# Attention and ternary feed-forward on one core: loads and angle tables of chunk 0 reordered, sums directly behind their values

## The chip, the cores and the metric

The kernel runs on one core of a Trainium2 chip. The metric is the device time of one execution in microseconds (us). The engines are TensorE (PE; weight loads are listed apart as PEld), VectorE (DVE), ScalarE (ACT), GpSimd (POOL) and SyncE (SP), which here only issues DMAs; ScalarE issues some too.

## The reference

```python
xn = layernorm(x)                            # x: 2048 x 256, no scale, no shift
q, k, v = xn@Wq, xn@Wk, xn@Wv                # 8 query heads, 2 key/value heads, 32 wide
q, k = rope(q), rope(k)                      # angles from tables over the 2048 rows
std = softmax(causal(q@k.T * 32**-0.5)) @ v
qp, kp = q[..., :3]@dirs, k[..., :3]@dirs    # one number per row and head
geo = softmax(causal(qp[:, None]*kp[None, :])) @ v
attn = (std + head_scales*(geo - std)) @ Wo
z = xn @ ternary(W_syn).T + b_syn            # 1024 wide; ternary: mean(|W|)*{-1,0,1}
hidden = where(z >= 102nd largest of the row, relu(z), 0)
ffn = layernorm(xn + hidden@ternary(W_out).T + b_out)*gamma + beta
out = x + attn + ffn
```

## The kernel before

The 2048 rows are cut into four chunks of 512 rows, four tiles of 128 each. Nothing is looped at run time. `build_plan` lists every piece of work with an engine, a length, what it needs, and a rank; then it repeatedly takes, among the pieces that could start within `SLACK` (120 ns) of the first, the one of lowest rank. The result is a written order for each of the five engines' queues. `LANDING` and `done` are its assumed landing times of DMAs; they set the order and no time on the chip. Each engine works through its queue in order and waits on semaphores.

For each chunk: statistics of x (`stat`, `eps`, `shift`, L1010 to L1027), normalised rows (`xn`, L836), their transposes (`xT`, `xnT`), three projections with the rope halves of queries and keys kept apart (`qA`, `qB`, `qK`, L1291) and the values (L1295). The cosines and sines come as tables of 16 and 32 numbers a row. `spread_angles` (L555 to L564) repeats them over the heads, in three pieces a chunk; TensorE transposes a piece (`tT`, four transposes, L1276), ScalarE copies it out (`t_put`, L827). Chunk 0's pieces go to `trig`; those of the later chunks go to `trig_next`, are parked in DRAM (`t_park`, L593) and come back (`trig_in`, L599) when the ropes of the chunk before are done. The angles, the given weights, the spread pieces and `trig_next` lie in `probs`, the buffer of the exponentials, so all trig work ends before the first exponential.

The rope products (L1065 to L1072) and the joins (L1078, L736, L739) give queries and keys, which are split into a high and a low part (`khi`, `hi` on ScalarE; `klo`, `lo` on VectorE, L1088 and L1093), parked in DRAM and read back as stacks (L627, L630) of 96 rows. From them come the pieces of the row maxima (`S`, L1312; reduced on VectorE, L1126 and L1129), a transpose (`mT`) and the maxima (`m`), which go into the stack as two more rows. The geometric scores need only small rows: `gx` (L1303, L1304), `geo_hi`, `geo_lo`, the running maxima (`scan`, `geo_top`), and some 22 small DMAs.

Attention goes by slots: chunk, kind (geometric first, then standard), group of four heads, key block of 128. A slot is two pairs of scores (L1395, L1399), two exponentials (L889) into one of two halves of `probs`, on the diagonal two cuts (L746), then values (`val`, L1413) and sums (`sum`, L1420), both column-tiled into `acc`. The exponentials of slot n+2 wait for the sums of slot n. Ranks are 12 for scores, 13 for values, 12.5 for sums. Two PSUM banks (`side`) serve everything else; row-maximum pieces may also use the four score banks while no scores can run. In the order that results, 120 of the 160 sums have other work between them and their values, and TensorE enters column-tiled work 172 times (counted in the order that `build_plan` writes).

The feed-forward weights are made ternary early (`w_abs`, `wsum`, `w_cut`, `wT`, `w_put`), W_out after W_syn in the same buffer (`w_next`, L679). The feed-forward tiles (`z`, `sign`, `pick`, `hT`, `fo`, `y`) fill gaps and run mostly beside chunks 2 and 3.

## Time and profile before

| | |
|---|---|
| device time, median of 3 | 775.68 us (774.01 to 776.37) |
| the profiled execution, its own time | 776.62 us |
| its span in the trace | 774.9 us |
| busy, share of the span | PE 90%, DVE 64%, ACT 58%, POOL 29% |
| granted TensorE clock, mean | 0.927 of full |
| DMA moved | 35.46 MB |

The busy time of an engine is the time in which one of its instructions ran. The granted clock is a share of full speed: 1.0 is 2.4 GHz, 0.5 is 1.2 GHz. In a timeline a row gives start, length, engine, line, operation, written and read tile, shapes and count, and in brackets the idle time before it with what ended it. A matmul's length contains its fill and drain, so start-to-start times are read for what it costs. Consecutive like instructions are merged into one row.

### The profile page before, as it was taken

How to read it: one execution, taken by the hardware profiler on the slowest of the kernel's cores; microseconds unless marked ns; L12 is line 12 of the kernel's file. 1: busy time of each engine (PE TensorE's matmuls, PEld its weight loads, DVE VectorE, ACT ScalarE, POOL GpSimd, SP SyncE). 2: the span in 40 equal slices, each digit the busy share in tenths (PEclk: the TensorE clock that was granted, in tenths of full speed). 3: DMA queues.
4: the chain of work that ended last, by engine and by line, in shares of the span. 5: the costliest groups of instructions: out<-in, count | busy, mean ns of one | idle time of the engine just before them, and what ended most of it. 6: DMA issues, size and time to landing. Idle time of an engine off the chain costs nothing.

```text
span 774.9 us, 12300 instructions
## 1 busy us (share of the span) xinstructions
PE 694.9 (90%) x4424; PEld 327.5 (42%) x4424; DVE 498.3 (64%) x974; ACT 449.4 (58%) x733; POOL 226.8 (29%) x304
## 2 busy tenths in 40 slices
PE   0857988799999999969999999999999989998993
PEld 0533444334244443423343444554544445654532
DVE  3782786856675876558567696567665567767602
ACT  1655345344334442468444445799989989996550
POOL 3431314531111212111010120452343453247232
PEclk9965899679899998989999999999989999999996
DMA  9494038240000000160000000000000000000000
GB/s 238 150 280 134 1 128 209 77 102 1 1 7 1 1 1 1 32 158 1 0 3 3 1 1 3 22 22 28 28 22 22 28 22 28 16 22 8 1 1 27
DMA packets 26931, 35.46 MB, mean 46 GB/s; under 512 B 7090, under 2 KB 21298, under 8 KB 26483
## 3 DMA queue, kind: packets, MB, share of 16 engines
q1 hardware_dynamic: 21874, 33.80, 15.0%
q10 hardware_dynamic: 4992, 0.84, 0.6%
q8 instruction: 36, 0.59, 0.3%
q14 instruction: 29, 0.23, 0.1%
HBM read 20.08 MB, written 13.89 MB: 44 GB/s over the span
## 4 chain that ended last, share of the span: by engine, by line
PE 62%; DVE 10%; issue 5%; ACT 3%; POOL 3%; DMA 3%; SPq 1%; DVEq 0%; ACTq 0%; POOLq 0%
PE acc L1420 14%; PE acc L1413 14%; PE side L1312 10%; PE scores L1395 7%; DVE piece_max L1126 4%; PE scores L1399 3%; DMA q_stack<-q_parked 3%; PE side L1366 2%; PE side L1357 2%; PE side L1374 2%; PE side L1367 2%; ACT probs L889 2%; PE side L1349 2%; PE side L1350 1%; POOL probs L746 1%
## 5 line engine op out<-in xcount | busy, mean ns | idle before, releaser
L889 ACT ACTIVATE probs<-scores 128x1024 f32<-128x1024 f32 (+3 forms) x320 | 271.0, 893 | 230.9 <-PE acc L1420 208.3
L1126 DVE TENSOR_REDUCE piece_max<-side 128x1 f32<-128x512 f32 x189 | 125.3, 685 | 78.9 <-PE side L1312 77.5
L1413 PE MATMUL acc<-probs,v_nat 128*32 128x512 f32 (+3 forms) x1280 | 158.1, 568 | 8.7 <-POOL probs L746 8.5
L1420 PE MATMUL acc<-probs,ones_all 128*32 128x512 f32 (+3 forms) x1280 | 156.8, 564 | 0.0
L1312 PE MATMUL side<-k_stack,q_stack 96*128 96x512 f32 (+3 forms) x309 | 122.5, 450 | 17.0 <-DMA q_stack<-q_parked 9.2
L746 POOL TENSOR_SCALAR_AFFINE_SELECT probs<-probs 128x256 f32<-128x256 f32 x128 | 60.8, 484 | 243.8 <-ACT probs L889 242.5
L1312 PEld LDWEIGHTS side<-k_stack,q_stack 96*128 96x128 f32 x309 | 55.5, 199 | 106.2 <-issue 52.4
L1395 PE MATMUL scores<-q_stack,k_stack 98*128 98x512 f32 (+3 forms) x320 | 92.5, 393 | 1.5 <-ACT probs L889 1.3
L1129 DVE CUSTOM_DVE_ANT_0 side<-side,tail_mask 128x256 f32<-128x256 f32 (+3 forms) x120 | 57.7, 488 | 33.3 <-PE side L1312 32.8
L1413 PEld LDWEIGHTS acc<-probs,v_nat 128*32 128x32 f32 x1280 | 37.2, 114 | 86.9 <-issue 64.8
L1152 DVE RECIPROCAL d_raw<-d_raw 128x512 f32<-128x512 f32 x16 | 53.6, 3347 | 23.2 <-ACT o_raw L902 23.2
L1395 PEld LDWEIGHTS scores<-q_stack,k_stack 98*128 98x128 f32 x320 | 54.0, 194 | 33.6 <-ACT probs L889 23.8
L1399 PE MATMUL scores<-q_geo,k_geo 10*128 10x512 f32 (+3 forms) x320 | 58.0, 485 | 5.9 <-ACT probs L889 4.9
L1420 PEld LDWEIGHTS acc<-probs,ones_all 128*32 128x32 f32 x1280 | 29.9, 111 | 48.5 <-issue 45.7
L1399 PEld LDWEIGHTS scores<-q_geo,k_geo 10*128 10x128 f32 x320 | 23.6, 190 | 47.5 <-ACT probs L889 31.2
L785 POOL TENSOR_TENSOR y_rstd<-y_mv,minus_half 128x1 f32<-128x1 f32 x16 | 9.6, 600 | 106.5 <-DVE y_mv L1258 106.5
L1276 PE MATMUL side<-ident,probs 128*128 128x128 f32 x48 | 11.6, 403 | 25.4 <-ACT probs L559 18.8
L1247 DVE TENSOR_TENSOR h_split<-side,h_split 128x512 fp32r<-128x512 f32 x32 | 21.2, 681 | 18.8 <-ACT h_split L980 18.8
L1240 DVE SCALAR_TENSOR_TENSOR work<-z_buf,thresh 128x1024 f32<-128x1024 f32 x16 | 22.0, 1378 | 17.4 <-DVEq L1237 17.4
L1366 PE MATMUL side<-down_T,h_split 128*128 128x256 f32 x128 | 31.9, 288 | 1.0 <-DVE h_split L1247 1.0
L1367 PE MATMUL side<-down_T,h_split 128*128 128x256 f32 x128 | 30.9, 280 | 0.0
L1349 PE MATMUL side<-up_T,xs_hi 128*128 128x512 f32 x64 | 28.3, 442 | 0.5 <-DVE xs_lo L1184 0.3
(165 smaller groups left out, 911.1 us busy)
## 6 DMA issues: line engine op xcount, KB each, us to landing
q_stack<-q_parked SPq DMA_DIRECT2D x12, 512.0 KB, 8.0
q_parked<-turned SPq DMA_DIRECT2D x8, 512.0 KB, 3.0
trig_parked<-probs SPq DMA_DIRECT2D x3, 768.0 KB, 5.2
trig<-trig_parked SPq DMA_DIRECT2D x3, 768.0 KB, 4.3
res<-in_L_attn_x_dram SPq DMA_DIRECT2D x4, 512.0 KB, 8.9
x_parked<-xn SPq DMA_DIRECT2D x4, 512.0 KB, 3.2
xT_parked<-xnT SPq DMA_DIRECT2D x4, 512.0 KB, 5.2
xb<-x_parked SPq DMA_DIRECT2D x16, 128.0 KB, 2.0
```

What stands on the lines that cost most here:

```text
L746: nc.gpsimd.affine_select(out=tri, in_=tri, compare_op=ALU.is_ge, fill=0.0, base=0, pattern=[[0, 2], [1, P]], channel_multiplier=-1).then_ ...
L889: nc.scalar.activation(probs[:, slot % 2, pair, :, off:], scores[:, pair, :, off:], ACT.Exp, scale=ATT_SCALE if kind == 0 else 1.0).then_i ...
L1126: free(nc.vector.tensor_reduce(piece_max[:, h, p:p + 1], pt, AX.X, ALU.max), ("S",) + a)
L1129: free(nc.vector.tensor_tensor_reduce(pt[:, 0:ncol], pt[:, 0:ncol], tail_mask[:, CHUNK - ncol:], 1.0, -3.0e38, ALU.add, ALU.max, piece_max ...
L1152: nc.vector.reciprocal(d_raw[:], d_raw[:]).then_inc(recip_ready, 1)
L1312: last = nc.tensor.matmul(pt[:, 0:ncol], q_stack[0:STK, b, h, col:col + P], k_stack[0:STK, h // HG, CHUNK * p:CHUNK * p + ncol], start=Tru ...
L1366: nc.tensor.matmul(pt[:, 0:C], h_hi[:, i], down_T[:, i], start=(i == 0), stop=False)
L1367: last = nc.tensor.matmul(pt[:, 0:C], h_lo[:, i], down_T[:, i], start=False, stop=(i == NN - 1))
L1395: last = nc.tensor.matmul(dst[:, off:], k_stack[:, g, P * j:P * j + P], q_stack[:, b, HG * g + h, off:], start=True, stop=True)
L1399: last = nc.tensor.matmul(dst[:, off:], k_geo[rows, P * j:P * j + P], q_geo[rows, g, off:], start=True, stop=True)
L1413: nc.tensor.matmul(acc[D * h:D * h + D, 0, off:], v_nat[:, j, g], probs[:, slot_no[a] % 2, h // 2, h % 2, off:], start=(j == 0), stop=(j = ...
L1420: last = nc.tensor.matmul(acc[D * h:D * h + D, 1, off:], ones[:, 0:D], probs[:, slot_no[a] % 2, h // 2, h % 2, off:], start=(j == 0), stop ...
```

## The change

Five edits, most of them in `build_plan`. Loads: the weights are issued first on ScalarE, then the angles of chunk 0 alone; SyncE issues x of chunk 0 and the small table, waits for the weights, and then issues the rest. Tables: `angles` has its own buffer of one chunk, refilled by `ang_in` (two DMAs on SyncE) for each later chunk; the spread pieces lie in the key part of `turned`, so they wait until the chunk before is parked; every chunk's pieces go straight to `trig`, and the parked trig, its DMAs and `trig_next` are gone. Sums: their rank is -1, so a sum is taken right behind its values, and row-maximum pieces find their place at the scores only. The cut of w_cut in two: `w_mean` makes mean and thresholds and frees the bank, `w_cut` the ternary matrix, with a new semaphore `ternary_ready`. Order: geo work and the statistics from chunk 2 on wait for maxima; W_out, `xz_in` and `xb_in` come behind the stack of chunk 0; W_out's thresholds come behind its maxima.

```diff
-LANDING = {"m_dma": 2300, "geo_dma": 2300, "geo_rows": 2300, "w_next": 5000, "t_park": 3500, "trig_in": 3000, "xn_park": 3500,
+LANDING = {"m_dma": 2300, "geo_dma": 2300, "geo_rows": 2300, "w_next": 5000, "ang_in": 2500, "xn_park": 3500,
...
+SUM_RANK = -1
...
+W_UNIT = 1.5
...
+        if c:
+            add("ang", "sp", 2, ("ang_in", c), 1100, [("unit", "tT", c - 1, 2)])
...
-            rank = 0 if c == 0 else 0.5
-            add("spread", "act" if c == 0 else "pool", rank, ("spread", c, s), 650 if c == 0 else 1300, [("tables",)] + turned[-2:-1])
+            rank = 0 if c == 0 else 2 * c - 0.5
+            slots_free = [("khi_park", c - 1), ("klo_park", c - 1)] if c else []
+            add("spread", "act" if c == 0 else "pool", rank, ("spread", c, s), (650, 650, 900)[s] if c == 0 else (700, 700, 900)[s],
+                [("ang_in", c)] + turned[-2:-1] + slots_free)
...
-            add("trig", "act", rank, ("t_put", c, s), 600, [("unit", "tT", c, s)] + [("t_park", c - 1)] * (c > 1), empties=("tT", c, s))
+            add("trig", "act", rank, ("t_put", c, s), 600, [("unit", "tT", c, s)] + [("rope", c - 1, k) for k in "ABK"] * (c > 0),
+                empties=("tT", c, s))
...
-        if c:
-            add("t_park", "sp", 0, ("t_park", c), 550, [("t_put", c, s) for s in range(3)])
-    add("w_sort", "dve", 0, ("w_sort",), 2000, [("w",)])
+    add("w_sort", "dve", 0.2, ("w_sort",), 2000, [("w",)])
...
-            add("stat", "dve", STAT_RANK if c else 0, ("stat", t), 650, [("x", c)])
+            add("stat", "dve", STAT_RANK if c else 0, ("stat", t), 650, [("x", c)] + [("m", c - 2)] * (c > 1))
...
-        if c:
-            add("trig_in", "sp", 1, ("trig_in", c), 550, [("t_park", c)] + [("rope", c - 1, s) for s in "ABK"])
...
-            add("rope", "dve", 0 if c == 0 else ROPE_RANK, ("rope", c, s), 1250, [("unit", "q" + s, c)] + ([("trig_in", c)] if c else [("t_put", 0, s) for s in range(3)]) + parked,
+            add("rope", "dve", 0 if c == 0 else ROPE_RANK, ("rope", c, s), 1250, [("unit", "q" + s, c)] + [("t_put", c, i) for i in range(3)] + parked,
...
+        due = [("m", c - 1)] if c else []
...
-        add("geo", "dve", rank, ("geo_lo", c), 1220, [("geo_hi", c)] + old)
-        add("geo", "dve", rank, ("scan", c), 2800, [("geo_in", c)] + old)
+        add("geo", "dve", rank, ("geo_lo", c), 1220, [("geo_hi", c)] + old + due)
+        add("geo", "dve", rank, ("scan", c), 2800, [("geo_in", c)] + old + due)
...
-            add("w", "sp", 0, ("w_next",), 500, [("w_cut", 0)])
+            add("w", "sp", 0, ("w_next",), 500, [("w_cut", 0), ("stack_lo", 0)])
...
-        unit("w", 0, ("wsum", m), 60, [("w_abs", m)])
-        add("w", "dve", W_RANK, ("w_cut", m), 4400, [("unit", "wsum", m)] + [("w_put", 0, 3)] * m, empties=("wsum", m))
+        unit("w", W_UNIT, ("wsum", m), 60, [("w_abs", m)])
+        add("w", "dve", 2, ("w_mean", m), 560, [("unit", "wsum", m)] + [("m", 0)] * m, empties=("wsum", m))
+        add("w", "dve", W_RANK, ("w_cut", m), 3900, [("w_mean", m)] + [("w_put", 0, 3)] * m)
...
-            unit("w", 0, ("wT", m, i), 440, [("w_cut", m)])
+            unit("w", W_UNIT, ("wT", m, i), 440, [("w_cut", m)])
...
-        add("xz", "sp", 3, ("xz_in", t), 550, [("xnT_park", c)] + [("xs_lo", t - 2)] * (t > 1))
+        add("xz", "sp", 3, ("xz_in", t), 550, [("xnT_park", c), ("stack_lo", 0)] + [("xs_lo", t - 2)] * (t > 1))
...
-        add("xb", "sp", 3, ("xb_in", t), 550, [("xn_park", c)] + [("y", t - 2)] * (t > 1))
+        add("xb", "sp", 3, ("xb_in", t), 550, [("xn_park", c), ("stack_lo", 0)] + [("y", t - 2)] * (t > 1))
...
-                + ([("sum",) + slots[n - 2]] if n >= 2 else [("t_park", NCH - 1), ("w_sort",)]))
+                + ([("sum",) + slots[n - 2]] if n >= 2 else [("w_sort",)]))
...
-        add("val", "pe", 12.5, ("sum", c, g, kind, j), 15 + 860 * share, [("val", c, g, kind, j)], "columns")
+        add("val", "pe", SUM_RANK, ("sum", c, g, kind, j), 15 + 860 * share, [("val", c, g, kind, j)], "columns")
...
-    done = {("x", 0): 5500.0, ("x", 1): 11000.0, ("x", 2): 13500.0, ("x", 3): 15500.0, ("tables",): 9000.0, ("dir_in",): 14000.0}
-    done.update({("w",): 9000, ("late",): 24000, ("w_in", 0): 19000, ("w_in", 1): 19000})
+    done = {("x", 0): 5200.0, ("x", 1): 13000.0, ("x", 2): 19000.0, ("x", 3): 21000.0, ("ang_in", 0): 9500.0, ("dir_in",): 14000.0}
+    done.update({("w",): 11000, ("late",): 26000, ("w_in", 0): 18000, ("w_in", 1): 19000})
...
+        angles = sb("angles", [P, TPC, ANG])
+        spread = turned[:, :, 2].rearrange("p b (t m) -> p b t m", m=P)
...
-        angles = flat[:, 0:NT * ANG].rearrange("p (t a) -> p t a", a=ANG)
-        w_given = flat[:, NT * ANG:NT * ANG + KC * QKV].rearrange("p (k n) -> p k n", k=KC)
-        trig_next = flat[:, 3 * CHUNK:6 * CHUNK].rearrange("p (s t) -> p s t", s=3)
-        spread = flat[:, 6 * CHUNK:8 * CHUNK].rearrange("p (b t m) -> p b t m", b=2, m=P)
+        w_given = flat[:, 0:KC * QKV].rearrange("p (k n) -> p k n", k=KC)
...
-        trig_parked = nc.dram_tensor("trig_parked", [NCH, P, 3, CHUNK], F32, kind="Internal").ap()
...
-        trig_out = sem("trig_out")
-        trig_in = sem("trig_in")
...
+        ternary_ready = sem("ternary_ready")
...
-            buf, tiles = spread[:, spread_no[(c, s)] % 2], slice(TPC * c, TPC * c + TPC)
+            buf = spread[:, spread_no[(c, s)] % 2]
...
-                            angles[:, tiles, at:at + HALF, None].broadcast_to([P, TPC, HALF, H]))
+                            angles[:, :, at:at + HALF, None].broadcast_to([P, TPC, HALF, H]))
...
-                 angles[:, tiles, 0:HALF, None].broadcast_to([P, TPC, HALF, G]))
+                 angles[:, :, 0:HALF, None].broadcast_to([P, TPC, HALF, G]))
...
-                        angles[:, tiles, :, None].broadcast_to([P, TPC, ANG, G]))
+                        angles[:, :, :, None].broadcast_to([P, TPC, ANG, G]))
...
+            sp.dma_start(small[:], small_table.broadcast_to([P, H * 3 + RANKS])).then_inc(dir_in, 16)
+            sp.wait_ge(w_in, N_W_IN)
...
-            sp.dma_start(small[:], small_table.broadcast_to([P, H * 3 + RANKS])).then_inc(dir_in, 16)
...
-                if k == "t_park":
+                if k == "ang_in":
...
-                    for s in range(3):
-                        consumed(sp, ("tT", c, s))
-                    sp.dma_start(trig_parked[c], trig_next).then_inc(trig_out, 16)
-                if k == "trig_in":
-                    c = key[1]
-                    sp.wait_ge(trig_out, 16 * c)
-                    for s in "ABK":
-                        consumed(sp, ("q" + s, c - 1))
-                    sp.dma_start(trig[:], trig_parked[c]).then_inc(trig_in, 16)
+                    sp.wait_ge(side_full, unit_no[("tT", c - 1, 2)] + 1)
+                    rows = slice(CHUNK * c, CHUNK * c + CHUNK)
+                    sp.dma_start(angles[:, :, 0:HALF], cos_table[rows, 0:HALF].rearrange("(t p) d -> p t d", p=P)).then_inc(ang_in, 16)
+                    sp.dma_start(angles[:, :, HALF:], sin_table[rows].rearrange("(t p) d -> p t d", p=P)).then_inc(ang_in, 16)
...
-                    consumed(sp, ("wsum", 0))
+                    sp.wait_ge(ternary_ready, 1)
...
-                    pool.wait_ge(ang_in, 32)
+                    pool.wait_ge(ang_in, 32 * (c + 1))
+                    pool.wait_ge(hi_out, 32 * c)
+                    pool.wait_ge(lo_out, 32 * c)
...
-            act.dma_start(angles[:, :, 0:HALF], cos_table[:, 0:HALF].rearrange("(t p) d -> p t d", p=P)).then_inc(ang_in, 16)
-            act.dma_start(angles[:, :, HALF:], sin_table.rearrange("(t p) d -> p t d", p=P)).then_inc(ang_in, 16)
...
+            act.dma_start(angles[:, :, 0:HALF], cos_table[0:CHUNK, 0:HALF].rearrange("(t p) d -> p t d", p=P)).then_inc(ang_in, 16)
+            act.dma_start(angles[:, :, HALF:], sin_table[0:CHUNK].rearrange("(t p) d -> p t d", p=P)).then_inc(ang_in, 16)
...
-                    if c > 1:
-                        act.wait_ge(trig_out, 16 * (c - 1))
-                    free(nc.scalar.copy(trig[:, s] if c == 0 else trig_next[:, s], pt), ("tT",) + a)
+                    if c >= 1:
+                        for q_ in ("qA", "qB", "qK"):
+                            consumed(act, (q_, c - 1))
+                    free(nc.scalar.copy(trig[:, s], pt), ("tT",) + a)
...
-                        act.wait_ge(trig_out, 16 * (NCH - 1))
...
-                        consumed(act, ("wsum", 0))
+                        act.wait_ge(ternary_ready, 1)
...
-                        consumed(act, ("wsum", 1))
+                        act.wait_ge(ternary_ready, 2)
...
-            mark(nc.vector.memset(other[KROWS:, 2], 0.0))
...
-                    if c == 0:
-                        for i in range(3):
-                            consumed(dve, ("tT", 0, i))
-                    else:
-                        dve.wait_ge(trig_in, 16 * c)
+                    for i in range(3):
+                        consumed(dve, ("tT", c, i))
+                    if c >= 1:
...
+                if k == "w_mean":
+                    m = a[0]
+                    pt = filled(dve, ("wsum", m))
+                    free(nc.vector.tensor_scalar(w_scale[:, m:m + 1], pt[:, 0:1], 1.0 / (N * C), None, ALU.mult), ("wsum", m))
+                    consumed(dve, ("wsum", m))
+                    link(nc.vector.tensor_scalar(w_cut[:, 0:1], w_scale[:, m:m + 1], 1e-8, 0.5, ALU.add, ALU.mult))
+                    link(nc.vector.tensor_scalar(w_cut[:, 1:2], w_cut[:, 0:1], -1.0, None, ALU.mult))
...
-                    pt = filled(dve, ("wsum", m))
...
-                    link(nc.vector.tensor_scalar(w_scale[:, m:m + 1], pt[:, 0:1], 1.0 / (N * C), None, ALU.mult))
-                    link(nc.vector.tensor_scalar(w_cut[:, 0:1], w_scale[:, m:m + 1], 1e-8, 0.5, ALU.add, ALU.mult))
-                    link(nc.vector.tensor_scalar(w_cut[:, 1:2], w_cut[:, 0:1], -1.0, None, ALU.mult))
+                        dve.wait_ge(down_in, 16)
+                    else:
+                        dve.wait_ge(up_in, 16)
...
-                    free(nc.vector.scalar_tensor_tensor(w_neg, w_raw, w_cut[:, 0:1], w_neg.bitcast(F32), ALU.is_gt,
-                                                        ALU.subtract), ("wsum", m))
+                    nc.vector.scalar_tensor_tensor(w_neg, w_raw, w_cut[:, 0:1], w_neg.bitcast(F32), ALU.is_gt,
+                                                   ALU.subtract).then_inc(ternary_ready, 1)
...
-                        consumed(pe, ("wsum", m))
+                        pe.wait_ge(ternary_ready, m + 1)
```

## Rows read from the trace of the kernel before

**Rows 1.** The page's part 1: busy us, share of the span, instructions.
```profile
PE 694.9 (90%) x4424; PEld 327.5 (42%) x4424; DVE 498.3 (64%) x974; ACT 449.4 (58%) x733; POOL 226.8 (29%) x304
```

**Rows 2.** Stages: window, length, busy us of each engine, granted clock, DMA share, GB/s.
```profile
0.00:65.00 65.00, 31.78 (x121) 20.68 (x121) 41.76 (x93) 28.69 (x51) 22.98 (x32) 0.84 0.78 228
...
98.50:133.20 34.70, 30.28 (x165) 15.08 (x161) 26.38 (x40) 17.09 (x28) 12.93 (x15) 1.00 0.59 163
...
175.00:490.00 315.00, 302.22 (x1843) 127.86 (x1845) 218.37 (x426) 149.34 (x204) 48.47 (x77) 0.95 0.05 13
490.00:700.00 210.00, 202.56 (x1468) 103.44 (x1468) 135.34 (x258) 191.00 (x367) 86.28 (x108) 0.98 0.08 24
```

**Rows 3.** Timeline of ScalarE, the first spread.
```profile
18.05 1.14 ACT L559 COPY probs<-probs 128x512 f32<-128x512 f32 x2 [4.20 <-DMA probs<-in_sin_table_dram]
```

**Rows 4.** Timeline of VectorE, 0 to 50 us.
```profile
5.19 0.43 DVE L1016 BATCH_NORM_STATS2 stats<-res 128x6 f32<-128x256 f32 x1 [0.21 <-DMA res<-in_L_attn_x_dram]
...
20.38 0.71 DVE L1032 COPY w_qkv<-probs 128x256 f32<-128x256 f32 x2 [12.31 <-DMA probs<-in_L_attn_Wv_dram]
...
35.10 0.69 DVE L1068 TENSOR_TENSOR turned<-side,trig 128x512 f32<-128x512 f32 x1
...
41.42 2.58 DVE L1171 SCALAR_TENSOR_TENSOR h_split<-z_buf,w_cut,h_split 128x2048 fp32r<-128x2048 f32 x1
...
44.52 1.21 DVE L1093 TENSOR_TENSOR turned<-turned 128x1024 fp32r<-128x1024 f32 x1
```

**Rows 5.** Timeline of TensorE, 28 to 65 us.
```profile
28.68 3.01 PE L1291 MATMUL side<-xnT,w_qkv 128*128 128x512 f32 x4
33.08 3.70 PE L1291 MATMUL side<-xnT,w_qkv 128*128 128x512 f32 x8 [1.38 <-DVE turned L1066]
...
41.43 1.91 PE L1304 MATMUL side<-turned,dirs_k 6*40 6x512 f32 x2
...
48.87 0.66 PE L1276 MATMUL side<-ident,probs 128*128 128x128 f32 x4
...
64.26 0.44 PE L1312 MATMUL side<-k_stack,q_stack 96*128 96x128 f32 x1 [2.92 <-DMA q_stack<-q_parked]
```

**Rows 6.** DMA issues: count, KB each, median us from issue to landing.
```profile
q_stack<-q_parked SPq DMA_DIRECT2D x12, 512.0 KB, 8.0
...
z_buf<-in_L_ffn_W_out_dram SPq DMA_DIRECT2D x1, 1024.0 KB, 5.3
...
probs<-in_sin_table_dram ACTq DMA_DIRECT2D x1, 256.0 KB, 16.7
...
probs<-in_L_attn_Wv_dram ACTq DMA_DIRECT2D x1, 64.0 KB, 8.7
```

**Rows 7.** Groups of instructions by line: busy us, mean ns, idle before.
```profile
L827 ACT COPY probs<-side 128x512 f32<-128x512 f32 x9 | 5.1, 583 | 11.2 <-PE side L1276 5.9 <-issue 4.8 <-PE side L1291 0.3
```

**Rows 8.** Timelines of VectorE and TensorE, chunk 3's last split and first piece.
```profile
328.82 1.21 DVE L1093 TENSOR_TENSOR turned<-turned 128x1024 fp32r<-128x1024 f32 x1
...
344.27 1.19 PE L1312 MATMUL side<-k_stack,q_stack 96*128 96x512 f32 x2 [5.12 <-DMA q_stack<-q_parked]
```

**Rows 9.** Timeline of TensorE, like matmuls at 563 us and two slots at 742.
```profile
563.21 0.40 PE L1349 MATMUL side<-up_T,xs_hi 128*128 128x512 f32 x1
563.44 0.40 PE L1350 MATMUL side<-up_T,xs_lo 128*128 128x512 f32 x1
...
742.39 1.04 PE L1413 MATMUL acc<-probs,v_nat 128*32 128x512 f32 x8
743.25 1.04 PE L1420 MATMUL acc<-probs,ones_all 128*32 128x512 f32 x8
744.22 1.21 PE L1395 MATMUL scores<-q_stack,k_stack 98*128 98x512 f32 x4
745.36 1.07 PE L1413 MATMUL acc<-probs,v_nat 128*32 128x512 f32 x8
```

**Rows 10.** Waits: who waited for whom, us in total, times, longest.
```profile
ACT probs L889 <- PE acc L1420: 208.3, 91, 7.9
```

## The prediction

> **What bounds the kernel now.** I read the page's summary first [rows 1]: TensorE is busy 90% of the span and no other engine comes near. The table by stage [rows 2] says where it is not. In the first 65 us TensorE is busy 31.8 us while the DMA engines are busy 78%; later the DMA engines hardly matter. From 175 to 700 us TensorE is busy 302 of 315 and 203 of 210 us, so any work that is moved into that part costs its own length. ScalarE is nearly as full from 490 to 700 us (191 of 210), and there only. The end (a reciprocal, the mix, the last output matmuls) is the same in both kernels. So two things can matter: when attention starts, and what one slot (two pairs of scores, values, sums) costs TensorE afterwards.
>
> In the head I followed one chain through the timelines of the engines. The angles are on the chip at 18.05, when the first spread starts after a wait on the sine table [rows 3]; the weights at 20.38 [rows 4]. The first projection starts at 28.68, the second at 33.08, the second geo matmul ends at 43.34 [rows 5], the low half of the queries is split off from 44.52 to 45.73 [rows 4], and the stack lands at 64.26, where the first row-maximum piece starts [rows 5].
>
> **Part 1, the loads.** Before, SyncE issues x of chunk 0, x of chunk 1, the small table, W_syn and the rest of x at once, and ScalarE both angle tables (all 2048 rows) and then the weights. The sine table took 16.7 us from issue to landing, Wv 8.7 [rows 6]. After: x of chunk 0 and the small table, then SyncE waits for the three weights (384 KB), and ScalarE issues a quarter of the angle rows (96 KB) behind the weights. Queued behind SyncE's wait are x of chunks 1 to 3, W_syn and the late parameters. Their earliest readers, the statistics of chunk 1 and the absolute sums of W_syn, are on no chain before the second rope, and VectorE and ScalarE have room for them (41.8 and 28.7 busy of 65 us [rows 2]); without that cover a late W_syn would push its thresholding, 2.58 us of VectorE in its longer half [rows 4], into the row maxima.
>
> How early do the angles land? No row shows it. From below: x of chunk 0, 512 KB, is in at 5.19 [rows 4], and nearly as much again (480 KB) is now to come with it, so not before 7. From above: 8.7 us for the weights, as Wv took, and behind them a quarter of the sine table's 16.7, together 13. I take 9.7, nearer the lower end, because 1 MB at the 228 GB/s of the head [rows 2] is 4.4 us of transfer, on top of the 5 us in which x came. That is 8.4 us earlier (5 to 11). The Trainium skill speaks against such rows of 64 and 128 bytes: "DMA: Bandwidth & Descriptors", section "Why small descriptors are slow", says that a short descriptor carries a fixed overhead. If that alone set the landing, the quarter would pay its quarter of the old time, the upper end above. The trace agrees in so far as 256 KB of sine rows took longer than any other early load [rows 6].
>
> **Part 2, angles to first projection.** Before it took 10.6 us, from 18.05 to 28.68, nearly all ScalarE copies with TensorE transposes between. Three of the copies are trig pieces of chunk 1, 0.583 us each [rows 7], 1.8 us, which move later. The shift of chunk 0, which stood behind the weight sort on VectorE (from 20.38 [rows 4]), is no longer late; I give that 0.9. So 2.7 off: the projection at 17.6, **11.1 us earlier**. The weights must be sorted by then (2 us after they land); at 13 they still are.
>
> **Part 3, projection to split.** The second projection started 4.4 us after the first, after a wait for a rope to empty a bank, though the first took only 3.0 [rows 5]: the other side bank held a trig piece of chunk 1. The second rope ran at 35.10, behind statistics of chunk 1 [rows 4]. With both gone I take 1.6 us, the gap in front of the second rope. The thresholding of W_syn ended at 44.00 [rows 4], where the low halves could have begun at 43.34 [rows 5]: 0.6. So far 13.3 us.
>
> **Part 4, split to stack.** Before: 45.73 to 64.26, 18.5 us, with 1 MB of W_out (5.3 us to land) and 768 KB of trig issued in front of the stack loads, which took 8.0 us each in the median of all [rows 6]. The same step in chunk 3, without that company, is 330.03 to 344.27, 14.2 us [rows 8]. So 4.3 us off; 0 if the small geo issues on SyncE still set it, 6 if a whole W_out is saved. Attention starts **17.6 us earlier**, near 46.7 us.
>
> **Part 5, what moves into full time.** Twelve trig units stay twelve, but nine leave the head. Those of chunks 1 and 2 fall where TensorE has slack (30.3 busy of 34.7 us [rows 2]). A unit is four transposes, 0.66 us [rows 5]; chunk 3's three cost 2.0, and I add 0.6 for the others: 2.6 us, from 2.0 to 6 x 0.66 = 4.0. The copies on ScalarE stay as many, and chunk 3's come before 490 us. Gone are the 4.6 MB written to and read from the parked trig, and their waits; three angle loads of 96 KB take their place. New waits: the spread on GpSimd waits for the parks of the chunk before, with the cuts of the diagonal blocks queued behind it, for which the values wait; the trig copy on ScalarE waits for the ropes before, with exponentials behind it. The written order knows both, so I price them at 0, and at up to 5.3 us, a landing, if it misjudges one. W_out's thresholding and its sixteen transposes, and the scans and geo rows of a chunk, go behind row maxima: same length, later, 0; chunk 0's maxima gain by it what chunk 1 pays.
>
> **Part 6, sums directly behind values.** In the order that the planner writes for the kernel before, 120 of the 160 sums do not directly follow their values, and TensorE enters a stretch of column-tiled work 172 times. After it is at most 160. What an entry and its exit cost is in [rows 9]: from values to the sums behind them 0.86 us start to start, but from sums to the scores behind them 0.97; four score matmuls in front of values 1.14, against 0.23 each, 0.92, between like matmuls of 512 columns. That is 0.11 + 0.22 = 0.3 us a stretch, and 12 fewer give 3.6 us. The Trainium skill, "TensorEngine Tiling (Array Packing)", section "Key Properties", says that a change of tiling mode drains the array; the trace agrees, with these 0.3 us. The ends of the term: 0 if the stretches stay 172, and 10 us if pieces that no longer split values from sums also find their banks ready.
>
> Sum: 17.6 - 2.6 + 3.6 = 18.6 us off 776.6, the profiled execution's own time (span 774.9 and 1.7 around it): 758.0. That execution was 0.9 above the median of the runs shown, so I say **757**.
>
> **The rivals.**
> *A, the head gives only part.* The geo chain (two scans, the products, the small issues on SyncE) takes the place of the stack loads, or the weights land late. Then only parts 1 and 2 carry: 776.6 - 11.1 + 2.6 - 1 = 767. For it: the head consists of nearly equal chains. Against it: all of them hang on the same projection.
> *B, more than I sum.* ScalarE waited 208 us for sums to release its buffers [rows 10], and sums come sooner by a pair of scores. If the slots tighten (10 us instead of 3.6 in part 6) and the head gives its best in parts 1 and 4 (2.6 + 1.7) and 3 us in chunk 1's stack: 758 - 13.7 = 744.
> *C, slower.* Scores now stand one sum, 0.86 us, later. Where ScalarE is full (490 to 700 us) a late score is a late exponential, and nothing catches up. At 0.86 us a slot it has eaten 18.6 us after 22 slots, and chunk 3 has 64. At 35 slots: 758 + 30 = 788. Against it: ScalarE's longest wait is for sums, not for scores [rows 10].
> *D, no change.* One later wait absorbs the head's gain: 776. Nothing in the trace is tied to an absolute time, so this needs C at about 22 slots.
>
> **How the numbers follow.** Forecast (750 to 764) 0.52; A (764 to 773) 0.17; B (735 to 750) 0.19; D 0.04; C 0.08. The range holds the forecast and most of A and B: 741 to 771. Faster by over 0.3% (2.3 us, about what a measurement of this kernel tells from no change) is the first three, 0.88; same 0.04; slower 0.08.
>
> **What would show it.** Part 1: the first spread near 9.7. Part 2: the first projection near 17.6. Part 3: the second right behind the first. Part 4: the first piece near 46.7. Part 5: three trig units shortly before chunk 3's projections, and cuts that don't wait behind a spread. Part 6: nothing between values and sums, and less busy time of TensorE than 694.9 us. I am wrong if attention starts near 47 and the end does not move with it, if the scores wait for ScalarE after 490, or if the weights land after 15.

## The result, and the profile after

The changed kernel takes **796.18 us** in the median (794.75 to 797.35), the kernel before 776.02: ratio 1.0259, 95% interval 1.0233 to 1.0286. The forecast was 757, in a range of 741 to 771. It was wrong in size and in sign. The profiled execution took 794.75 us, its span is 792.9.

The page's part 1 and the table by stage, which answer to [rows 1, 2]:

```profile
PE 710.9 (90%) x4424; PEld 343.0 (43%) x4424; DVE 498.9 (63%) x973; ACT 449.4 (57%) x733; POOL 228.6 (29%) x304
```

```profile
0.00:65.00 65.00, 47.39 (x184) 25.49 (x188) 42.04 (x100) 30.83 (x52) 23.87 (x32) 0.84 0.69 204
98.50:133.20 34.70, 25.77 (x191) 13.08 (x190) 23.24 (x49) 16.23 (x26) 15.05 (x20) 0.84 0.06 20
175.00:490.00 315.00, 299.21 (x1793) 132.51 (x1785) 199.00 (x375) 159.62 (x229) 60.15 (x87) 0.90 0.11 30
490.00:700.00 210.00, 195.08 (x1336) 95.11 (x1335) 126.32 (x231) 154.37 (x274) 66.29 (x82) 0.93 0.06 19
```

TensorE has as many matmuls as before and is busy 16 us longer, at a lower clock. The first stage did gain: 47.4 busy us instead of 31.8. But from 490 to 700 us TensorE works 7.5 us less than before, and ScalarE, nearly full before, is busy 154 us instead of 191. Work comes late to it. Over the whole span TensorE's idle time is nearly what it was (82.0 us, 80.0 before), so the head's gain has been lost again later. Time lost at the half clock grew by 33 us (column "half" of the table below), and what is left, TensorE's work at full speed, shrank by 17.

The head, in the timelines of ScalarE, TensorE and VectorE, and the DMA issues (they answer to [rows 3, 5, 4, 6]):

```profile
7.10 1.14 ACT L561 COPY turned<-angles 128x512 f32<-128x512 f32 x2 [2.34 <-DMA angles<-in_sin_table_dram]
```

```profile
15.51 7.73 PE L1294 MATMUL side<-xnT,w_qkv 128*128 128x512 f32 x12 [0.77 <-ACT xnT L847]
...
26.82 1.05 PE L1306 MATMUL side<-turned,dirs_q 24*40 24x512 f32 x2 [0.24 <-ACT xnT L847]
...
49.97 0.51 PE L1402 MATMUL scores<-q_geo,k_geo 10*128 10x512 f32 x4 [0.65 <-DMA q_geo<-maxima]
50.41 0.44 PE L1315 MATMUL side<-k_stack,q_stack 96*128 96x128 f32 x2
```

```profile
30.43 1.21 DVE L1091 TENSOR_TENSOR turned<-turned 128x1024 fp32r<-128x1024 f32 x1
```

```profile
q_stack<-q_parked SPq DMA_DIRECT2D x12, 512.0 KB, 7.1
...
probs<-in_L_attn_Wv_dram ACTq DMA_DIRECT2D x1, 64.0 KB, 4.8
angles<-in_sin_table_dram ACTq DMA_DIRECT2D x1, 64.0 KB, 4.2
```

The angles are there at 7.10, the three projections run in one piece from 15.51, and attention starts at 50.0, now behind the small geometric DMA and no longer behind the stack. That is 14 to 15 us earlier than before.

The waits of the exponentials (who waited for whom, us in total, times, longest), to be laid beside the 208.3 of [rows 10]:

```profile
ACT probs L890 <- PE acc L1423: 146.9, 42, 6.9
ACT probs L890 <- PE scores L1402: 68.0, 36, 9.4
ACT probs L890 <- PE scores L1398: 49.0, 34, 9.4
```

Before, the two waits for scores were these:

```profile
ACT probs L889 <- PE scores L1399: 11.5, 15, 2.6
ACT probs L889 <- PE scores L1395: 10.6, 17, 2.2
```

ScalarE now waits 61 us less for sums and 95 us more for scores.

Where the head start goes can be read off the first scores of each chunk and kind in TensorE's timeline: the changed kernel is ahead by 15 us at chunk 0, 29 at chunk 1, 10 at chunk 2, 9 at chunk 3's geometric scores (487.9 against 497.2), 0 at its standard scores (629.5 against 629.3), and 18 behind at the last sum (773.3 against 755.2). The last row-maximum piece ends at 527.9, 51 us later than before (476.4), and the last feed-forward output (`fo`) starts at 783.6 instead of 734.2.

### The profile page after: what moved, and what is told of

It reads as the page before. It is cut to its first block, busy times and chain, and to the rows that moved or that the text cites. A ratio compares the mean times of both kernels' runs of the same rounds, so it can differ in the third digit from the quotient of the medians.

```text
span 792.9 us, 12318 instructions
## 1 busy us (share of the span) xinstructions
PE 710.9 (90%) x4424; PEld 343.0 (43%) x4424; DVE 498.9 (63%) x973; ACT 449.4 (57%) x733; POOL 228.6 (29%) x304
## 4 chain that ended last, share of the span: by engine, by line
PE 60%; DVE 12%; ACT 5%; POOL 5%; issue 4%; DMA 3%; SPq 0%; DVEq 0%; ACTq 0%; POOLq 0%
PE acc L1416 15%; PE acc L1423 13%; PE side L1315 11%; PE scores L1398 5%; DVE piece_max L1124 4%; PE scores L1402 4%; ACT probs L890 3%; DMA q_stack<-q_parked 2%; PE side L1377 2%; PE side L1369 2%; PE side L1370 2%; PE side L1352 1%; PE side L1294 1%; POOL probs L747 1%; PE side L1360 1%
## 5 line engine op out<-in xcount | busy, mean ns | idle before, releaser
L890 ACT ACTIVATE probs<-scores 128x1024 f32<-128x1024 f32 (+3 forms) x320 | 269.8, 893 | 264.7 <-PE acc L1423 146.9
L1416 PE MATMUL acc<-probs,v_nat 128*32 128x512 f32 (+3 forms) x1280 | 170.4, 608 | 11.5 <-POOL probs L747 10.5
L1124 DVE TENSOR_REDUCE piece_max<-side 128x1 f32<-128x512 f32 x190 | 126.5, 687 | 69.3 <-PE side L1315 67.0
L1423 PE MATMUL acc<-probs,ones_all 128*32 128x512 f32 (+3 forms) x1280 | 163.9, 587 | 0.0
L1315 PE MATMUL side<-k_stack,q_stack 96*128 96x512 f32 (+3 forms) x312 | 135.8, 482 | 18.9 <-DMA q_stack<-q_parked 5.5
L747 POOL TENSOR_SCALAR_AFFINE_SELECT probs<-probs 128x256 f32<-128x256 f32 x128 | 56.7, 453 | 214.0 <-ACT probs L890 212.5
L1315 PEld LDWEIGHTS side<-k_stack,q_stack 96*128 96x128 f32 x312 | 60.7, 209 | 104.8 <-issue 44.1
L1423 PEld LDWEIGHTS acc<-probs,ones_all 128*32 128x32 f32 x1280 | 45.2, 122 | 92.7 <-issue 90.4
L1416 PEld LDWEIGHTS acc<-probs,v_nat 128*32 128x32 f32 x1280 | 34.1, 118 | 80.6 <-issue 57.3
L1398 PEld LDWEIGHTS scores<-q_stack,k_stack 98*128 98x128 f32 x320 | 55.6, 196 | 25.0 <-ACT probs L890 17.6
L1369 PE MATMUL side<-down_T,h_split 128*128 128x256 f32 x128 | 33.3, 296 | 3.6 <-DVE h_split L1250 3.6
L1370 PE MATMUL side<-down_T,h_split 128*128 128x256 f32 x128 | 32.4, 289 | 0.0
L768 POOL TENSOR_TENSOR o_raw<-o_raw,d_raw 128x512 f32<-128x512 f32 x8 | 10.3, 1281 | 70.8 <-DVE d_raw L1150 70.8
L1369 PEld LDWEIGHTS side<-down_T,h_split 128*128 128x128 f32 x128 | 25.2, 197 | 9.2 <-issue 4.6
```

The costliest lines, as they stand in the source:

```text
L747: nc.gpsimd.affine_select(out=tri, in_=tri, compare_op=ALU.is_ge, fill=0.0, base=0, pattern=[[0, 2], [1, P]], channel_multiplier=-1).then_ ...
L890: nc.scalar.activation(probs[:, slot % 2, pair, :, off:], scores[:, pair, :, off:], ACT.Exp, scale=ATT_SCALE if kind == 0 else 1.0).then_i ...
L1124: free(nc.vector.tensor_reduce(piece_max[:, h, p:p + 1], pt, AX.X, ALU.max), ("S",) + a)
L1315: last = nc.tensor.matmul(pt[:, 0:ncol], q_stack[0:STK, b, h, col:col + P], k_stack[0:STK, h // HG, CHUNK * p:CHUNK * p + ncol], start=Tru ...
L1369: nc.tensor.matmul(pt[:, 0:C], h_hi[:, i], down_T[:, i], start=(i == 0), stop=False)
L1370: last = nc.tensor.matmul(pt[:, 0:C], h_lo[:, i], down_T[:, i], start=False, stop=(i == NN - 1))
```

## The experiments

Four theories stood at the start. **S**: the sums' rank of -1 costs by itself, since scores stand behind sums (rival C's mechanism). **P**: it costs by shutting row-maximum pieces out from between values and sums, and they pace the feed-forward. **K**: the lower granted clock is a cause of its own. **G**: the trig pieces' new place leaves a gap between the pieces of chunks 1 and 2. The table has all 18 runs; the edit is against the kernel named first. The ratio compares with the kernel before as it ran beside the run (its median there was 773.7 to 777.9 us), so it is the safer number between runs. The columns from "traced" on are of one execution, the profiled one, whose own time "traced" gives: in e1, e5, e10, e11 and e18 it is the slowest of its kernel's, in the changed kernel, e3, e14 and e15 the fastest, and a difference between two traces of a few us can be one between executions. "Last sum" and "last piece" are the ends of the last sum and of the last row-maximum piece, "last `fo`" is a start; idle is the span less TensorE's busy time in the page's part 1. "Half" is half of the busy time that fell into stretches with the half clock granted, an estimate of what that clock cost, summed over the records of the trace.

| run | edit | us (median) | ratio to before, 95% | traced | last sum | last piece | last `fo` | idle | half |
|---|---|---|---|---|---|---|---|---|---|
| before |  | 776.0 | 1 | 776.6 | 755.2 | 476.4 | 734.2 | 80.0 | 44.0 |
| after |  | 796.2 | 1.0233 to 1.0286 | 794.8 | 773.3 | 527.9 | 783.6 | 82.0 | 76.7 |
| e1 | after, sums 12.5 | 769.6 | 0.9905 to 0.9970 | 775.9 | 754.5 | 488.9 | 727.5 | 59.5 | 65.7 |
| e2 | before, sums -1 | 800.4 | 1.0259 to 1.0370 | 801.0 | 772.0 | 520.6 | 791.1 | 97.4 | 70.6 |
| e3 | after, -1 for geometric only | 794.8 | 1.0207 to 1.0307 | 791.7 | 769.9 | 517.3 | 771.7 | 78.8 | 66.8 |
| e4 | after, -1 for standard only | 778.6 | 1.0013 to 1.0071 | 780.2 | 759.7 | 518.6 | 761.6 | 70.2 | 63.2 |
| e5 | after, sums 9 | 787.7 | 1.0130 to 1.0164 | 789.2 | 768.5 | 473.6 | 739.6 | 74.4 | 73.2 |
| e6 | e1, trig early | 778.4 | 1.0010 to 1.0064 | 778.4 | 757.3 | 478.1 | 721.5 | 69.7 | 55.3 |
| e7 | after, light search | 788.3 | 1.0124 to 1.0193 | 790.5 | 769.7 | 526.7 | 779.8 | 78.2 | 77.1 |
| e8 | e1, light search | 765.5 | 0.9841 to 0.9888 | 766.9 | 746.0 | 487.1 | 718.9 | 55.1 | 60.4 |
| e9 | after, 32 rows | 786.6 | 1.0103 to 1.0190 | 785.3 | 763.4 | 521.9 | 773.8 | 82.8 | 63.3 |
| e10 | e1, 32 rows | 765.4 | 0.9817 to 0.9902 | 767.2 | 746.6 | 480.8 | 719.5 | 62.4 | 49.9 |
| e11 | before, new loads | 768.6 | 0.9843 to 0.9951 | 774.7 | 754.5 | 472.3 | 733.6 | 69.3 | 54.3 |
| e12 | before, 32 rows | 778.2 | 0.9948 to 1.0083 | 776.4 | 754.9 | 476.1 | 734.0 | 80.5 | 43.3 |
| e13 | after, sums 11.5 | 792.0 | 1.0159 to 1.0256 | 791.0 | 770.2 | 472.0 | 722.0 | 73.1 | 68.0 |
| e14 | before, sums 11.5 | 828.2 | 1.0637 to 1.0695 | 822.0 | 800.5 | 475.0 | 739.8 | 94.0 | 75.5 |
| e15 | e11, 32 rows | 769.5 | 0.9895 to 0.9950 | 766.6 | 745.1 | 466.3 | 724.1 | 70.3 | 43.4 |
| e16 | after, scores first | 787.7 | 1.0150 to 1.0196 | 784.0 | 746.7 | 501.3 | 773.7 | 76.0 | 66.4 |
| e17 | e1, scores first | 765.7 | 0.9866 to 0.9922 | 764.8 | 743.0 | 481.0 | 730.6 | 59.5 | 53.1 |
| e18 | e17, 32 rows | 766.4 | 0.9865 to 0.9915 | 767.9 | 746.3 | 484.0 | 733.9 | 61.5 | 57.5 |

**The sums' rank, undone and done alone.**

```diff
-SUM_RANK = -1
+SUM_RANK = 12.5
```

> The changed kernel with the sums' rank back at 12.5, everything else of the change kept. Theory S (the sums' rank is the cause of the 20 us): the head's 15 us stay and the loss goes, 775.7 - 15 + 2 = about 762, granted clock back near 0.92, half-speed time near 115 us instead of 171. Theory R (the rest of the change is the cause: deferred pieces, trig units and W_out's thresholding in full time): within 5 us of the changed kernel, 791 to 801, whatever the sums do.

> The kernel before with one number changed: rank -1 for the sums. Theory S: slower than before by the loss without the head's gain, 775.7 + 15 + 20 = about 811, granted clock near 0.89, first piece still at 64 us. Theory R: 776 or a little less, 772 to 776, because 128 turns fewer at 0.15 us each can only help.

The one number takes 25 to 27 us off the changed kernel and makes it faster than the kernel before; alone it costs the kernel before 24 us. Theory S had the direction; its sizes, 762 and 811, were both missed (769.6 and 800.4). Everything else in the change together gives 6.5 us by the medians, 2 to 7 by the interval. In e1 ScalarE waits for sums as before (206 us), and for scores 49 us, between the 22 of before and the 117 of the changed kernel:

```profile
ACT probs L890 <- PE acc L1423: 206.1, 85, 7.9
...
ACT probs L890 <- PE scores L1402: 32.9, 19, 10.6
...
ACT probs L890 <- PE scores L1398: 15.7, 22, 3.0
```

**Which kind of attention.** The sum's rank became `SUM_RANK if kind == 1 else 12.5` in e3, `kind == 0` in e4.

> The changed kernel with rank -1 for the geometric kind only, 12.5 for the standard kind. If the loss is made where ScalarE and the feed-forward share the geometric stretches, and where most drops of the granted clock start, this keeps most of it: 785 to 796. If it is made in the standard stretches, or evenly, 762 to 780. Theory R again: 791 to 801.

> The counterpart: rank -1 for the standard kind only. If the geometric stretches make the loss, 762 to 770; if the standard ones make it, 785 to 796; if each gives its half, both this and the counterpart near 778. Theory R: 791 to 801.

The geometric kind alone carries the 25 us, the standard kind alone 9. Together they cost little more than the first, so they seem to share a limit; which one, these two runs don't show, and the 9 us of e4 lay outside both of its forecasts.

**Pieces between values and sums again.** Rank 9 lets row-maximum pieces (rank 7 at most) in, and nothing of rank 10 and above.

> The changed kernel with the sums' rank at 9: row-maximum pieces (ranks 1 to 7) may again stand between values and sums, scores (12) and feed-forward units (10, 11) may not. Theory P (the loss is the slower pace of the row-maximum pieces, which delays the feed-forward chain that follows them to the end): the last piece comes back from 527 to near 488 us and the time to 768 to 778. Theory T (the loss is in the scores that come one sum later, or in the lower clock of longer column-tiled stretches, whoever stands between): only a part comes back, 782 to 796.

8.5 of 27 us come back. Theory P, as the whole, falls: the last piece is back at 473.6 and the feed-forward is done by 740, but attention still ends at 768.5.

**Trig early, and a lighter search.** e6 gives the trig of the later chunks rank 0.5 on top of e1. In e7 and e8 the search for the threshold reads 64 of the 1024 columns and has no fallback.

> The changed kernel with the sums' rank at 12.5 (769.6 us) and the trig units of chunks 1 to 3 back at rank 0.5, ahead of the row-maximum pieces. Theory G (the head's 15 us shrink to 6 because chunk 2's trig units, ranked behind chunk 1's pieces, hold up chunk 2's projections and leave 40 us without pieces): the gap between chunk 1's and chunk 2's pieces closes, the last piece comes 10 to 25 us sooner than 488, the time 755 to 764. Rival (the head's gain goes into time at the lower clock, 150 us against 115): the gap closes and the time stays at 767 to 772.

> The changed kernel in its own order, with the threshold search of the feed-forward on 64 of 1024 columns: the three sign passes, the compare, both maxima and the replacement between them; its fallback is left out. The other feed-forward work stays. Theory P: the feed-forward tiles, 15 us each after the last piece, no longer set the end; it moves with the attention, below 770. Theory T: TensorE sets the end with or without the search, 785 to 793.

> The same reduction in the changed kernel with the sums' rank at 12.5. Theory P: little changes against its 769.6, since its attention ends last anyway, 758 to 768, and the distance to the counterpart with sums behind values falls from 26 us to under 10. Theory T: the distance stays above 18.

e6 is 9 us slower than e1, outside both of its forecasts: G falls, the new place of the trig is the better one. The light search leaves 23 of 27 us between sums behind and sums free, so ScalarE's and VectorE's load in the search isn't the limit.

**The clock.** The geometric scores contract over 10 rows of 32; in the other 22 the queries hold zeros (the keys -1), so 32 rows give the same sums:

```diff
-                            rows = slice(32 * h, 32 * h + 2 * GROWS)
+                            rows = slice(32 * h, 32 * h + 32)
```

> The changed kernel in its own order; the geometric scores contract over all 32 rows of their row tile instead of 10. Rows 10 to 31 hold -1 against 0, so the result is the same and the streamed columns are the same. Theory K (the clock falls because the order leaves TensorE with little activity, and geometric scores on 10 of 32 rows are the least of it): half-speed time falls from 171 us to under 140 and the time by 8 to 16 us, 780 to 788. Theory T (waits and order alone): 794 to 798, half-speed time 160 to 180.

> The same 32 rows in the changed kernel with the sums' rank at 12.5 (769.6 us, 150 us at half speed). Theory K: 755 to 764, half-speed time under 130. Theory T: 767 to 772.

> The kernel before with the 32 rows alone. Theory K: 44 us are lost to half speed in its trace by my count, about a third of it inside geometric stretches, so 762 to 772 and half-speed time under 100 us. Theory T: 774 to 778.

On the changed kernel it gives about 9 us, on e1 4 to 6 (between its two forecasts), on the kernel before nothing. K holds for part of the loss there, not in general (e15 and e18, below). The pair e10 and e9 also repeats e1 and the changed kernel with 32 rows in both: the sums' rank still costs 21 of 27 us.

**The loads alone,** on the order of before: weights first, SyncE's wait, the angle rows of chunk 0 in front of the rest.

> The kernel before in its own written order, with the loads of the change alone: weights first, SyncE waiting for them before x of chunk 1, angle rows of chunk 0 ahead of the others. The first spread starts at 8 to 10 us instead of 18. If a head start carries to the end, the time falls by what the first piece gains: by 5 to 9 us (the weight sort, not the angles, may then set the first projection), 767 to 771. If the clock or a later wait takes it back, 774 to 777.

7.5 us faster: as much as the whole change gives with its sums free (6.5). Its four executions are worth a look one by one: with a mean granted clock of 0.929 they took 765.8 and 766.7 us, with 0.920 770.5, with 0.914 774.7, and the last one is the traced one.

**Scores behind sums, and nothing else shut out.** Rank 11.5 leaves feed-forward units (10, 11) and pieces in front of sums, as 12.5 does; only the scores (12) change places with them.

> The changed kernel with the sums at rank 11.5: row-maximum pieces and all feed-forward units may still stand between values and sums, as at rank 12.5, and only the scores (rank 12) now stand behind a sum where both could go. 487 mode changes in the written order against 497 at 12.5 and 362 at -1. Of the 25 us between 769.6 (12.5) and 794.8 (-1), rank 9 kept 18 (787.7). Theory L (late scores: a sum in front of scores costs by itself, whatever else may stand there): most of those 18 us are here too, 782 to 790. Theory F (the feed-forward units lose their place between values and sums, and that is what the exponentials miss): the loss is in the step from 11.5 to 9, and this run stays at 768 to 774.

> The kernel before with nothing but the sums' rank, 12.5 to 11.5: sums in front of scores, all other units in front of sums as they were. 496 mode changes against 482 and 40 to 61 sums directly behind their values. Theory L: 787 to 795, most of the 24 us that rank -1 cost here (800.4). Theory F: 774 to 780.

The direction is theory L's, with 22 and 52 us; the sizes are not, 792.0 against at most 790 and 828.2 against at most 795. e14, one rank moved by one, is the slowest run of all, though its feed-forward is done by 740. By the planner's rule a score now waits for a sum and for every unit in front of that sum; why that costs here twice what it costs the changed kernel is open. Its waits:

```profile
ACT probs L889 <- PE acc L1420: 166.2, 55, 9.1
...
ACT probs L889 <- PE scores L1399: 58.2, 27, 7.0
...
ACT probs L889 <- PE scores L1395: 33.2, 25, 3.5
```

> The kernel before with the reordered loads (768.6 alone) and geometric scores that contract over 32 rows (778.2 alone, so nothing by itself, yet 4 us on the changed kernel with free sums and 8 to 10 on the changed kernel). Clock theory: the wider contraction helps where the geometric chunk comes earlier and meets half-speed time: 762 to 766. If it is only noise between orders: 768 to 771.

769.5 is e11 again: a miss for K. That "half" is 43.4 here and 54.3 in e11 is no effect of the rows: e11's trace is its slowest execution (774.7 us), this one's its fastest (766.6), and e11's executions at the same mean clock took as long. The wide difference is one stretch of 27 us at the half clock from 328 us on, which e11's trace has and this one lacks.

**Sums behind values, but scores first.** The values of a slot get one more need in the planner:

```diff
+            + ([("score",) + slots[n + 1] + (PAIRS - 1,)] if n + 1 < len(slots) and slots[n + 1][0] == c else []), "columns")
```

> The changed kernel with sums at rank -1, all 160 directly behind their values, and one more need in the planner: the values of a slot come only when both pairs of scores of the next slot are written (within a chunk). Counted in the written order: a pair of scores stands only 2 times where no more than two pairs ran ahead of the values (40 times in the changed kernel, 22 in the one before, 15 with free sums, 67 in the 828 us run), 393 mode changes (362 changed, 482 before). Theory L (a score behind values and sums is what costs, not the closeness of values and sums): 764 to 776, near the free sums' 769.6. If instead closeness itself costs (pieces and feed-forward units shut out, exponentials released in bursts), it stays at 785 to 795.

> The same need with the sums at rank 12.5: 48 sums directly behind their values, 498 mode changes, 2 scores late. Theory L: as good as the free sums or somewhat better, 762 to 770. If late scores are not it: 769.6 again, or worse where values now wait.

> The run above with geometric scores contracting over 32 rows, which took 4 us off free sums (769.6 to 765.4): 758 to 766 if both help, the fastest of all; above 768 if one undoes the other.

e16 missed theory L's forecast (764 to 776) and met its rival's (785 to 795): with the scores safe, closeness of values and sums still costs. It is the most telling run. Its last sum comes at 746.7, 27 us sooner than in the changed kernel and sooner than in e1, so the order of scores decides much of when attention ends; ScalarE's waits for scores fell less than that suggests, from 117 us to 96. But its time is 787.7, because behind attention stands a feed-forward that isn't done. TensorE's timeline at its end:

```profile
743.71 1.94 PE L1361 MATMUL side<-ident,work 128*128 128x128 f32 x8 [3.06 <-DVE work L1244]
...
746.01 0.65 PE L1424 MATMUL acc<-probs,ones_all 128*32 128x128 f32 x8
...
757.68 6.47 PE L1378 MATMUL side<-w_o,mixed 128*128 128x256 f32 x16 [5.30 <-issue]
...
767.07 1.94 PE L1361 MATMUL side<-ident,work 128*128 128x128 f32 x8 [2.79 <-DVE work L1244]
...
770.50 0.55 PE L1370 MATMUL side<-down_T,h_split 128*128 128x256 f32 x1 [1.49 <-DVE h_split L1251]
```

From the last sum to the end it takes 35 us instead of 20, with a whole tile's search and transposes behind the output matmuls. With the sums free (e17) the same need gives 765.7, by the ratio 3 us better than e1, which the intervals (0.9866 to 0.9922 and 0.9905 to 0.9970) don't quite tell from nothing. 32 rows add nothing to that (e18).

## Why the prediction was wrong

**Part 1 was right, and better.** The first spread at 7.10, forecast 9.7. **Part 2 too:** first projection at 15.51, forecast 17.6. **Part 3 held:** the three projections follow without a gap (7.73 us). **Part 4 gave nothing:** from the end of the split (31.64) to the first piece (50.41) it takes 18.8 us, against 18.5 before and 14.2 forecast, so attention starts at 50.0 and not at 46.7. The geometric scores stand first in the new order and waited for their DMA, as rival A had it; the stack loads took 7.1 us instead of 8.0.

**Part 5 was not measured by itself.** No cut waited behind a spread; the longest wait for a cut, 5.5 us at 125.8, was behind a mix.

**The carry of the head was over-sized.** Parts 1 to 5 were to bring 15 us (17.6 - 2.6). With the sums at their old rank they bring 6.5 (e1). Part of what is missing is the clock. Where it is as before's, a head start of the loads alone arrives whole: e15's trace starts its scores 10.2 us earlier than before's and ends 10.1 us earlier (span 764.8 against 774.9), with "half" as before (43.4 and 44.0); its 32 rows alone give nothing (e12).

```profile
65.08 0.80 PE L1399 MATMUL scores<-q_geo,k_geo 10*128 10x512 f32 x4 [0.38 <-DMA q_geo<-maxima]
```

```profile
54.84 0.80 PE L1402 MATMUL scores<-q_geo,k_geo 32*128 32x512 f32 x4 [0.42 <-DMA q_geo<-maxima]
```

The other edits lose some of theirs at any clock: e10 has a mean clock of 0.929, starts its scores 15.2 us earlier and ends 9.8 us earlier. And e1's ten executions took 766.6 to 775.9 us, the faster ones at a clock of 0.915 to 0.922, the slower at 0.905 to 0.914; its trace is the slowest, where 21 us less idle time than before are eaten by 22 us more in "half". Which of the other edits costs e10 its 5 us, and why e1 is granted less, is open.

**Part 6 is the step that failed.** It said that sums directly behind values save turns, 3.6 us, and priced what they push back at nothing. Measured, the sums' rank costs 24 to 27 us. That is some 30 us from forecast to measured, and with the 8.5 us of the head's carry it makes the 39 us between 757 and 796. The turns were right in kind and even under-sized. TensorE's work at full speed (span less idle less "half") fell from 648.5 us in e1 to 634.2 after, with 362 mode changes in the written order instead of 497, and from 650.9 to 631.3 between before and e2 (482 to 354): 0.11 and 0.15 us a change. The stretch of like work in two slots shows it, the answer to [rows 9]:

```profile
743.44 1.07 PE L1416 MATMUL acc<-probs,v_nat 128*32 128x512 f32 x8
744.33 1.04 PE L1423 MATMUL acc<-probs,ones_all 128*32 128x512 f32 x8
745.18 1.04 PE L1416 MATMUL acc<-probs,v_nat 128*32 128x512 f32 x8
746.04 1.04 PE L1423 MATMUL acc<-probs,ones_all 128*32 128x512 f32 x8
```

Values, sums, values, sums, 0.86 us each and no turn. But this is also the fault. I had counted 160 stretches of column work for 160 slots; the planner wrote 98, because in 63 slots the values follow those of the slot before with no score between (22 before, 25 in e1; 62 in e2, 58 in e13, 65 in e14, 56 in e5). Every order with over 40 of these, e3, e4 and e16 among them (43, 42, 41), is slower than the kernel before; that is a count beside the times, not a cause shown. The stretch from 506 to 532 us has two such blocks of four in the changed kernel. Here it is for that kernel, then for e1 (busy us of PE, PEld, DVE, ACT, POOL, clock, DMA share, GB/s):

```profile
506.00:532.00 26.00, 25.25 (x138) 10.70 (x142) 13.18 (x26) 10.27 (x12) 3.62 (x3) 0.93 0.01 2
```

```profile
506.00:532.00 26.00, 25.84 (x184) 13.58 (x177) 16.30 (x37) 21.45 (x40) 9.13 (x12) 1.00 0.10 30
```

TensorE is full in both. ScalarE is busy 10 us in the one and 21 in the other, but not with exponentials. Those alone (L890), in the same order:

```profile
506.00:532.00 26.00, 9.69 (x10) 0.93 0.01 2
```

```profile
506.00:532.00 26.00, 10.12 (x11) 1.00 0.10 30
```

In this stretch attention is as fast in both. What ScalarE lacks in the changed kernel is feed-forward work: TensorE still makes row-maximum pieces, which ended at 488.9 in e1. TensorE's timeline of the changed kernel there, and ScalarE's:

```profile
510.95 1.07 PE L1416 MATMUL acc<-probs,v_nat 128*32 128x512 f32 x8
511.83 1.04 PE L1423 MATMUL acc<-probs,ones_all 128*32 128x512 f32 x8
512.69 1.04 PE L1416 MATMUL acc<-probs,v_nat 128*32 128x512 f32 x8
513.55 1.04 PE L1423 MATMUL acc<-probs,ones_all 128*32 128x512 f32 x8
514.52 3.72 PE L1377 MATMUL side<-w_o,mixed 128*128 128x256 f32 x16
...
518.40 0.51 PE L1402 MATMUL scores<-q_geo,k_geo 10*128 10x512 f32 x4
```

```profile
513.00 1.94 ACT L890 ACTIVATE probs<-scores 128x1024 f32<-128x1024 f32 x2 [3.96 <-PE acc L1423]
518.94 1.94 ACT L890 ACTIVATE probs<-scores 128x1024 f32<-128x1024 f32 x2 [3.99 <-PE scores L1402]
```

The exponentials of one slot wait for the sums at 511.83; behind the block comes other work, the next scores start at 518.40, and ScalarE stands still for 3.99 us. Over this stretch attention lost nothing by it, as the two counts show. In e1 a pair of scores goes between, and the sums that are not yet due stand behind it:

```profile
511.70 1.07 PE L1423 MATMUL acc<-probs,ones_all 128*32 128x512 f32 x8
512.58 1.04 PE L1416 MATMUL acc<-probs,v_nat 128*32 128x512 f32 x8
513.55 1.09 PE L1360 MATMUL side<-ident,work 128*128 128x128 f32 x8
514.57 0.81 PE L1402 MATMUL scores<-q_geo,k_geo 10*128 10x512 f32 x4
515.31 1.06 PE L1423 MATMUL acc<-probs,ones_all 128*32 128x512 f32 x8
516.19 1.04 PE L1416 MATMUL acc<-probs,v_nat 128*32 128x512 f32 x8
```

So there are two mechanisms, each shown in a pair of runs. Scores behind sums delay attention: e13 differs from e1 by that alone (11.5 for 12.5), its feed-forward is done 5 us sooner, and its last sum comes at 770.2 instead of 754.5. Work shut out from between values and sums delays the feed-forward: e16 differs from e17 by that, attention ends nearly alike (746.7 and 743.0), and the last `fo` starts at 773.7 instead of 730.6 and sets the end. Which work it is, e5 and e13 tell. Letting the row-maximum pieces back in (rank 9) brings the last piece from 527.9 to 473.6 and the last `fo` from 783.6 to 739.6; letting the units of rank 10 and 11 in as well (rank 11.5) brings it to 722.0. So theory P was wrong as the whole and right for the larger part of this half. The changed kernel has both (773.3 and 783.6), and they don't add; I read this as the work that one delays filling the gaps that the other leaves, but no run shows it.

In what form the time is lost can be told in part. From free to close sums (e1 to after, e10 to e9, e17 to e16, before to e2) idle time grows by 16 to 23 us and "half" by 11 to 27, while the rest shrinks by 10 to 20, which I put down to the turns. So the lower clock carries a good part, in e2 and e14 (31.5 us over before) more than the idle time. It comes with the order in every execution: the mean granted clock is 0.890 to 0.894 in the changed kernel and 0.905 to 0.922 in e1. What the order would cost at an equal clock, no run shows.

**The rivals.** C was right in mechanism and in sign, and its 788 is the nearest number of all; I gave it 0.08. Two things I held against it were read wrongly. "ScalarE's longest wait is for sums, not for scores" is true of the order before, where scores came first: the wait that is short shows what that order protects, not what is cheap to give up. And I looked for C where ScalarE was full, 490 to 700 us, while e13 is 24 us behind e1 before that, at chunk 3's first geometric scores (506.7 against 482.2). Most of the loss is made by the geometric kind alone (e3); why that kind, no run shows. The prediction also priced Part 6 by counting stretches without running the rank through the planner's rule: a sum at -1 beats everything that could start with it, the scores and the feed-forward too, not only the pieces.

## What to carry to other kernels

When a queue's order is changed to save turns, list all that now stands behind the moved work, and ask for each who waits for it; a wait that is near zero in the profile may be the one that the order was keeping at zero. Then list what the moved work shuts out (here the row-maximum pieces), and what hangs on that at the end. Count turns in the order as it will be written and not by the number of slots. Before two traces are compared, look where each stands among its kernel's executions: here one kernel's spread over 9 us, with the granted clock.

## What the runs showed of the hardware

Three things that I had not expected. One kernel is granted different clocks in different executions, and its time follows: e11 took 765.8 and 766.7 us at a mean of 0.929, 770.5 at 0.920 and 774.7 at 0.914, e1 766.6 at 0.922 and 775.9 at 0.905. In the changed kernel the time lost at the half clock was 76.7 us, against 44.0 before, with TensorE busy 90% of the span in both; the lowest of the stages I read is from 50 to 118.6 us, chunk 0's attention:

```profile
50.00:118.60 68.60, 60.26 (x364) 28.48 (x365) 50.81 (x133) 30.96 (x50) 22.84 (x44) 0.75 0.25 71
```

Contracting over 32 rows instead of 10 costs TensorE next to nothing (3 to 4 us more work at full speed, 0 on the kernel before). It took 13 us of "half" from the changed kernel (76.7 to 63.3) with 9 us of time, and 16 from e1 (65.7 to 49.9) with 4 to 6, where a part is e1's slow traced execution; on the kernel before, on e11 and on e17 it changed no time that can be told. What decides that is open.

And a change of tiling mode costs 0.11 to 0.15 us by the totals above, an estimate, 0.2 to 0.3 us a stretch, in and out. The Trainium skill, "TensorEngine Tiling (Array Packing)", section "Key Properties", says that such a change drains the array. The runs agree in that each change costs time, and set the size: 135 changes fewer gave 14 us, and the order that saved them cost 25.
